# Laying queries with two transfers and keys with four, the keys' requested by ScalarE, in a four-layer attention kernel

## What is computed

```python
qkv = x_norm @ W_qkv + b_qkv
attn_w = jax.nn.softmax(jnp.einsum('bhqd,bhkd->bhqk', q, k) * scale, axis=-1)
attn_out = jnp.einsum('bhqk,bhkd->bhqd', attn_w, v)
x = x + gate_a[:, None] * (attn_out @ W_proj + b_proj)
q_c = _ln(x) @ W_qc + b_qc
kv_c = _ln(context) @ W_kvc + b_kvc
...
x = x + c_attn_out
h = jax.nn.gelu(modulate(_ln(x), shift_m, scale_m) @ W_mlp1 + b_mlp1)
x = x + gate_m[:, None] * (h @ W_mlp2 + b_mlp2)
```

## Time and profile before

| | |
|---|---|
| median of 3 runs | 2543.25 us (2536.22 to 2543.28) |
| the profiled execution, its own time | 2544.03 us |
| its span in the trace | 2542.2 us |
| TensorE (PE) busy | 2426.0 us, 95% |
| VectorE (DVE) busy | 1862.8 us, 73% |
| ScalarE (ACT) busy | 1271.5 us, 50% |
| GpSimd (POOL) busy | 468.1 us, 18% |

### The profile page before, as it was taken

The page is one execution under the profiler, slowest core; times in us unless marked ns, Lnnn a source line. Parts: engine busy times, 40 slices in busy tenths (PEclk is TensorE's granted clock), DMA queues, the critical chain, the costliest instruction groups (busy, mean ns, idle before and its releaser), DMA issues.

```text
span 2542.2 us, 94053 instructions
## 1 busy us (share of the span) xinstructions
PE 2426.0 (95%) x41410; PEld 1606.8 (63%) x41410; DVE 1862.8 (73%) x3532; ACT 1271.5 (50%) x1810; POOL 468.1 (18%) x510
## 2 busy tenths in 40 slices
PE   5779999999999999999999999999999999999998
PEld 3456666666666666666666666656666666666665
DVE  4677777777777878877767767767777777777762
ACT  1245544555555555554554555554544555545443
POOL 0111211212112111111211211212211212112121
PEclk8889999999999999999999999999999999999999
DMA  5422222222222322232122122122232222222211
GB/s 192 130 95 79 79 75 76 76 85 92 82 80 79 94 85 90 75 103 74 53 78 75 59 76 75 60 91 89 77 94 84 83 84 68 90 74 82 84 37 39
DMA packets 236858, 209.35 MB, mean 82 GB/s; under 512 B 87682, under 2 KB 222020, under 8 KB 236452
## 3 DMA queue, kind: packets, MB, share of 16 engines
q1 hardware_dynamic: 236452, 203.32, 25.2%
HBM read 58.34 MB, written 4.39 MB: 25 GB/s over the span
## 4 chain that ended last, share of the span: by engine, by line
PE 70%; DVE 15%; SPq 4%; issue 4%; ACT 4%; DMA 2%; POOL 1%; DVEq 0%; POOLq 0%; ACTq 0%
PE ring L1218 30%; PE score L1325 10%; PE o_acc L1378 9%; PE ring L1214 8%; PE score L1347 7%; DVE row_max_F L1006 6%; DVE row_max_G L1006 5%; PE ring L1172 3%; ACT probs L1145 3%; PE score L1352 2%; DMA k_F<-k_parts 2%; SPq L680 2%; SPq L690 1%; SPq L689 1%; DVE x_hat_E L861 1%
## 5 line engine op out<-in xcount | busy, mean ns | idle before, releaser
L1145 ACT ACTIVATE probs<-score 120x2048 f32<-120x2048 f32 (+1 forms) x320 | 601.8, 1881 | 348.5 <-PE score L1352 343.1
L1006 DVE TENSOR_REDUCE row_max_F<-score 128x8 f32<-128x2048 f32 x192 | 438.7, 2285 | 81.9 <-PE score L1325 79.4
L1006 DVE TENSOR_REDUCE row_max_G<-score 128x16 f32<-128x1920 f32 x128 | 276.1, 2157 | 117.0 <-PE score L1325 116.9
L1156 ACT ACTIVATE h_t<-ring,cols 128x256 f32<-128x256 f32 x384 | 160.7, 470 | 327.4 <-PE ring L1218 289.0
L1218 PE MATMUL ring<-w_fc,h_t 128*32 128x256 f32 x5184 | 310.0, 384 | 0.0
L1028 DVE STREAM_TRANSPOSE o_turned<-o_acc 128x512 f32<-128x512 f32 x224 | 159.9, 714 | 193.5 <-PE o_acc L1378 190.3
L1218 PE MATMUL ring<-x_t_E,w_fc 128*32 128x256 f32 x4640 | 273.5, 380 | 0.0
L1218 PEld LDWEIGHTS ring<-w_fc,h_t 128*32 128x32 f32 x5184 | 160.2, 111 | 107.2 <-issue 3.4
L1218 PEld LDWEIGHTS ring<-x_t_E,w_fc 128*32 128x32 f32 x4640 | 145.9, 110 | 98.7
L1378 PE MATMUL o_acc<-probs,v_self 128*17 128x256 f32 x3072 | 203.8, 383 | 0.0
L821 POOL TENSOR_TENSOR x<-x,gated 128x256 f32<-128x256 f32 x96 | 70.5, 734 | 721.7 <-DVE gated L1060 721.7
(11 more groups left out here) (150 smaller groups left out, 4054.7 us busy)
## 6 DMA issues: line engine op xcount, KB each, us to landing
q_G<-q_parts SPq DMA_DIRECT2D x256, 128.0 KB, 2.1
q_F<-q_parts SPq DMA_DIRECT2D x192, 128.0 KB, 2.1
k_F<-k_parts SPq DMA_DIRECT2D x96, 256.0 KB, 2.5
k_F<-k_parts SPq DMA_DIRECT2D x192, 128.0 KB, 2.3
k_G<-k_parts SPq DMA_DIRECT2D x128, 120.0 KB, 2.2
k_G<-k_parts SPq DMA_DIRECT2D x256, 60.0 KB, 2.0
gate_now_P<-gate_rows SPq DMA_DIRECT2D x48, 256.0 KB, 3.3
gate_now_E<-gate_rows SPq DMA_DIRECT2D x48, 256.0 KB, 3.5
```

What stands on the lines that cost most here:

```text
L1006: nc.vector.tensor_reduce(dst, src, AX.X, ALU.max).then_inc(row_max_ready[r].sem, 1)
L1145: nc.scalar.activation(probs[v % 2][0:keys, :, :], score[0:keys, :].rearrange("p (h q) -> p h q", h=2 * GROUPS), ACT.Exp, scale=SCALE).the ...
L1156: last = nc.scalar.activation(h_t[:, c, :], ps[:, c % 2 * NT:(c % 2 + 1) * NT], ACT.Gelu_apprx_tanh, bias=col(m, "fc1", c))
```

## The change

Three things change. A query job is laid by two transfers that read both parts, a key job by four. For this the buffers are laid out with the pair index `e` ahead of the chunk `c`, so that a partition's 512 (or 240) numbers are contiguous on both sides; the odd partitions of the second copy of the keys come from the parts read backwards (`::-1`). The products read the same numbers at the same widths from the new places. And the keys' transfers are asked for by ScalarE: in its list `steps_a` it meets `K.d` and `KV.d`, waits for VectorE's low parts, and issues four transfers. SyncE lays queries only.

```diff
     steps = [e for e in every if not e[2].endswith(".d")]
+    steps_a = [e for e in every if not e[2].endswith(".d") or e[2] in ("K.d", "KV.d")]
...
-        q = {r: [sb(f"q_{r}{i}", [P, KC, 2, NT]) for i in range(2)] for r in "FG"}
-        k_two = {"F": [sb(f"k_F{i}", [P, 2, KC, 2, NT]) for i in range(2)],
-                 "G": [sb(f"k_G{i}", [P, 2, KC, 2, S]) for i in range(2)]}
+        q = {r: [sb(f"q_{r}{i}", [P, 2, KC, NT]) for i in range(2)] for r in "FG"}
+        k_two = {"F": [sb(f"k_F{i}", [P, 2, 2, KC, NT]) for i in range(2)],
+                 "G": [sb(f"k_G{i}", [P, 2, 2, KC, S]) for i in range(2)]}
...
-        k_parts = sb("k_parts", [P, 2, KC, NT])
+        k_parts = sb("k_parts", [P, 2 * KC * NT])
...
-        Q_MOVES, K_MOVES = 4, 6
+        Q_MOVES, K_MOVES = 2, 4
...
+        def k_planes(r):
+            width = NT if r == "F" else S
+            return k_parts[:, 0:2 * KC * width]\
+                .rearrange("p (t c n) -> p t c n", t=2, c=KC)
...
                 for e in range(2):
-                    for part in range(2):
-                        sp.dma_start(q_now[part:P:2, :, e, :], q_parts[e:P:2, part, :, :]).then_inc(q_laid, 16)
-
-            def lay_k(r, m, n):
-                sp.wait_ge(k_parts_ready[r].sem, k_parts_ready[r].after(m, n))
-                t_psum[r].wait_before(sp, m, n, len(k_two[r]))
-                k_now = buffer(k_two, r, m, n)
-                width = NT if r == "F" else S
-                for e in range(2):
-
-                    sp.dma_start(k_now[0:P:2, :, :, e, :], k_parts[e:P:2, :, :, 0:width]).then_inc(k_laid, 16)
-                    sp.dma_start(k_now[1:P:2, 0, :, e, :], k_parts[e:P:2, 1, :, 0:width]).then_inc(k_laid, 16)
-                    sp.dma_start(k_now[1:P:2, 1, :, e, :], k_parts[e:P:2, 0, :, 0:width]).then_inc(k_laid, 16)
+                    sp.dma_start(q_now[:, e, :, :].rearrange("p c n -> p (c n)"),
+                                 q_parts[e:P:2, :, :, :].rearrange("p t c n -> p t (c n)")).then_inc(q_laid, 16)
...
-                elif step in ("K", "KV"):
-                    lay_k(attends[r], m, n)
...
-            for r, m, step, n, here in steps:
+            def lay_k(r, m, n):
+                act.wait_ge(k_parts_ready[r].sem, k_parts_ready[r].after(m, n))
+                t_psum[r].wait_before(act, m, n, len(k_two[r]))
+                k_now = buffer(k_two, r, m, n)
+                planes = k_planes(r).rearrange("p t c n -> p t (c n)")
+                for e in range(2):
+                    for two in range(2):
+                        parts = planes[e:P:2, ::-1, :] if two else planes[e:P:2, :, :]
+                        act.dma_start(k_now[:, two, e, :, :].rearrange("p c n -> p (c n)"), parts).then_inc(k_laid, 16)
+
+            for r, m, step, n, here in steps_a:
                 ps = ring[here] if here is not None else None
+                if step in ("K.d", "KV.d"):
+                    lay_k(attends[r], m, n)
+                    continue
```

More of the change, by code:

```diff
@@ L972, in _ @@
                 elif step == "K":
-                    low_parts(k_parts, k_high_ready, k_parts_ready, "F", m, n, ring[here], "qkv", KC, NT)
+                    low_parts(k_planes("F"), k_high_ready, k_parts_ready, "F", m, n, ring[here], "qkv", KC, NT)
                 elif step == "V":
@@ L987, in _ @@
                         dve.wait_ge(*cross_biases_loaded(m)[0])
-                    low_parts(k_parts, k_high_ready, k_parts_ready, "G", m, n, ring[here], "kv", 0, S)
+                    low_parts(k_planes("G"), k_high_ready, k_parts_ready, "G", m, n, ring[here], "kv", 0, S)
                     pv_psum["G"].wait_before(dve, m, n, len(v_one["G"]))
@@ L1115, in _ @@
                     parts, high, jobs, laid, moves = ((q_parts, q_high_ready, q_jobs, q_laid, Q_MOVES) if step == "Q" else
-                                                      (k_parts, k_high_ready, k_jobs, k_laid, K_MOVES))
+                                                      (k_planes(f), k_high_ready, k_jobs, k_laid, K_MOVES))
                     done = {"Q": q_psum.get(r), "K": k_psum, "KV": kv_psum}[step]
@@ L1325, in _ @@
                                     last = mm(score[:, col0:col0 + width],
-                                              q_now[at, c, e, tile * P:(tile + 1) * P].bitcast(F32R),
-                                              k_now[at, two, c, e, :].bitcast(F32R), start=two == 0, stop=two == 1)
+                                              q_now[at, e, c, tile * P:(tile + 1) * P].bitcast(F32R),
+                                              k_now[at, two, e, c, :].bitcast(F32R), start=two == 0, stop=two == 1)
                     last.then_inc(s_psum[r].sem, 1)
@@ L1347, in _ @@
                                 mm(score[0:keys, g * BANK + e * NT:g * BANK + (e + 1) * NT],
-                                   k_now[at, two, c, e, tile * P:tile * P + keys].bitcast(F32R),
-                                   q_now[at, c, e, :].bitcast(F32R), start=two == 0, stop=False)
+                                   k_now[at, two, e, c, tile * P:tile * P + keys].bitcast(F32R),
+                                   q_now[at, e, c, :].bitcast(F32R), start=two == 0, stop=False)
                         for g in range(GROUPS):
```

## The result

The changed kernel takes 2723.07 us (median of 4 runs, 2720.86 to 2730.64), the kernel before 2539.73 us (median of 4, 2535.95 to 2543.28): a ratio of 1.0724 (95% interval 1.0699 to 1.0748), 183 us slower. The forecast was 2667 us, range 2605 to 2700. The direction and the way were right, and the time lies above the range.

The account below looks back on a forecast made before the run. TensorE was taken to bound the kernel. Stalls of 46, 20.5 and 56 us from ScalarE's key issues, 122.5 us in all, on the profiled 2544.03 us gave 2666.5, predicted as 2667 us, range 2605 to 2700.

Parts of the forecast that it names:

- The bound: Whole kernel: TensorE, with 70% of the chain that ended last, sets the time; idle time forced on it adds up.
- what the key wait is worth: ScalarE's wait for key transfers before overwriting k_parts, turns without layer 1: a perfect cure is worth 16.7 us, 0.7%.
- An issue holds ScalarE 0.65 us: ScalarE's list behind each key job: each transfer issue holds its queue 0.65 us, 2.6 us for four.
- The price taken as the lowest: Lower bound for an issue: 0.33 us, a gate load from DRAM of another shape, or 0.38 us with 0.05 added.
- The rule of the Trainium skill: Issuing from several engines saves only sequencer time, usually small; by it neither gain nor loss would be large.
- The stalls: TensorE waiting behind cross-attention key issues: 46 us in 19 turns, 20.5 in ten, 56 in fifteen, 122.5 us together.
- the matmuls' busy time the same: Changed profile, TensorE: the busy time of the matmuls was expected to stay unchanged.
- Start and end at 0: Eight key jobs of the hand-written start and end: put at 0, at worst 21 us.
- Cheap issues: Rival: issues on ScalarE cost 0.38 us each, 48 us less in 44 turns, 2619 us; chance 0.10.
- overlap: Rival: only the wait for low parts holds ScalarE, issues run beside its work; +10.6 us, 2555 us; chance 0.11.
- the faster case: Rival: the exponential is not held by the low parts either, only the key wait's end remains; 2527 us; chance 0.06.

Follow-up runs that it names:

- experiment 1: Changed kernel with the new layout, but SyncE asks for the keys' transfers and ScalarE's wait for the low parts is gone: 2519.47 us, 0.992 of the kernel before.
- experiment 4: New layout with SyncE issuing the keys' transfers, but ScalarE still waits for VectorE's low parts at K.d and KV.d: 2547.64 us, 1.0031 of the kernel before.
- Experiment 3: Changed kernel plus 24 unused transposes on TensorE ahead of F.T3's scores in the 25 turns without layer 1: 2686.27 us, 1.0582 of the kernel before.
- experiment 5: Changed kernel, but without layer 1 two of the four cross-attention key issues stand behind F.T3's exponential: 2659.8 us, 1.048 of the kernel before.
- experiment 7: Changed kernel, but cross-attention key issues moved behind E.LN in turns with layer 1, early place kept in turns without: 2674.68 us, 1.0537 of the kernel before.

## Why the prediction was wrong, point by point

**The bound, and what the key wait is worth: right.** 16.7 us were said, and TensorE's wait fell by 16.7 when the new layout was laid by SyncE (experiment 1). The time fell by 20, because the clock gave something back as well; that term was missing here too.

**An issue holds ScalarE 0.65 us: right.** 0.63 us with 0.03 to the next, four in 2.5 us, and beside the activation ahead of them. The price taken as the lowest was misread: at its start the trace of before has issues from DRAM of 0.25 to 0.29 us (L654), below the 0.33 us of the gate load, which would move that rival a little lower and change nothing else. The rule of the Trainium skill weighed against the move ("DMA: Bandwidth & Descriptors", "Issuing engines are not separate DMA queues"), that sequencer time is usually small, would have made little of it; here ScalarE's issues cost 175 us (experiment 4 against the changed kernel).

**The stalls: right in place and number, within 15% in size.** Each turn, and the sum in us (the third row less the 1.7 us of before, the second less the 15.0 of before):

| turns | forecast | measured | sum forecast | sum measured |
|---|---|---|---|---|
| 19 with layer 1 | 2.4 | 2.1 | 46 | 40.0 |
| 10 without, no normed context | 3.55 | 3.48 | 20.5 | 34.8 - 15.0 = 19.8 |
| 15 without, normed context | 3.85 | 3.82 | 56 | 57.3 - 1.7 = 55.6 |

Together 122.5 us were forecast and 115.4 came. The last two are the waits of 1310 to 1810 us and of 1810 to 2590 us, in this order:

```profile
PE score L1353 <- ACT probs L1151: 34.8, 10, 3.7
```

```profile
PE score L1353 <- ACT probs L1151: 57.3, 15, 4.4
```

**The step that failed: "the matmuls' busy time the same".** The sum added TensorE's idle time and left its speed alone. It had no term for the granted clock, and that term is 60 us: 58.4 us more busy time, or 98 against 38 us by the clocks. Experiment 3 changes the clock without changing the lateness and gets 37 us back; experiments 5 and 7 show it rise and fall with the length of the stalls. The trace of before held the sign of it, and I didn't look. It has three waits of 2.7 us in the first ten of these turns, the longest of the earlier trace rows; two of them in its timeline:

```profile
1473.63 0.80 PE L1347 MATMUL score<-q_F,k_F 32*128 32x256 f32 x8 [2.69 <-ACT probs L1145]
...
1711.05 0.51 PE L1347 MATMUL score<-q_F,k_F 32*128 32x256 f32 x8 [2.66 <-ACT probs L1145]
```

And what followed them, in its windows (columns as above):

```profile
1473.60:1477.60 4.00, 3.97 (x48) 2.55 (x52) 0.94 (x3) 2.58 (x3) 0.00 (x0) 0.50 0.01 2
1711.00:1715.00 4.00, 3.95 (x56) 2.22 (x60) 0.97 (x3) 2.60 (x3) 0.00 (x0) 0.62 0.02 4
```

The clock is 0.50 and 0.62 behind them, one stretch at the lower level and one for most of it. Behind the third, which ended at 1379.25, the next 4 us were at 1.00. I forecast waits of 3.55 and 3.85 us, longer than any of these, in 25 turns. If each had cost what those 4 us at half clock did, 2 us, that would have been 50 us more, and a forecast of 2717. A lower clock did follow in 24 of the 25 turns.

**Start and end at 0: too low.** By the starts of VectorE's row maxima the changed kernel is 8 us behind at 217 us, and it loses about 7 more between 2600 and 2679 us, behind the last of the 44 turns, of which 1.5 are won back by the end. 115.4 + 60 + 8 + 5 = 188, against 186.6 us between the two spans. That it comes out so near is in part luck: some of the 8 and 5 may be clock, which the 60 already hold, and the freed key wait would take something off; these few us were not told apart.

**The rivals.** Cheap issues (2619) and overlap (2555) fell with the issue rows and with experiment 4; the faster case needs ScalarE to pass the issues, and it is what SyncE's issuing gives, not ScalarE's.

## What to carry to other kernels

When a change puts an idle time of some microseconds ahead of the engine that bounds the kernel, price it twice: once for its length, and once for the clock of what runs behind it, read from the windows behind the longest waits that the trace already has. An issue of 0.63 us belongs on an engine that nobody waits for; on a compute engine, look at what stands right behind it in the list, for where TensorE waits for that, four of them cost 2.5 us, and elsewhere little. A change with several parts is best timed in parts: here a gain of 20 us was hidden under a loss of 204.

## What the hardware showed that was not expected

- Short waits of TensorE in the middle of a kernel that is otherwise at 1.00 were followed by half the clock, the longer ones nearly always. The table counts the waits behind which the granted clock was below 1.00 somewhere in the next 8 us:

| TensorE's waits, us | where | how many | followed by a lower clock |
|---|---|---|---|
| 0.8 to 1.1 | experiment 4, turns without layer 1 | 25 | 0 |
| 0.65 to 1.8 | experiment 3, the same turns, behind the transposes | 25 | 1 |
| 2.0 to 2.8 | the changed kernel, turns with layer 1 | 19 | 5 |
| 2.1 to 3.0 | experiment 5, turns without layer 1 | 25 | 7 |
| 3.4 to 4.4 | the changed kernel, the same turns | 25 | 24 |

- The wait's length alone does not decide: of the three waits of 2.7 us in the kernel before, two were followed by a lower clock and one was not. What else does stays open. How much is lost behind one differs as well: 0.67, then 0.90 in the two stretches of 4 us behind the wait of 3.74 us shown above, 0.59, then 1.00 behind one of 3.42 at 1345.25.
- A transfer of 256 KB of `k_F` took 3.0 us from issue to landing when ScalarE asked for it and 2.6 us when SyncE did (experiment 1), where the old layout had 2.5. It is not simply the engine: the 256 KB of `q_G`, which SyncE asked for in both, took 3.0 and 2.7, and the 120 KB of `k_G` landed sooner when ScalarE asked, 2.1 against 2.5. Why was not looked into.
